# Decoder megakernel on one core: clearing the semaphores of a stage late and together instead of after every stage

## The reference

```
x = x + L0_attn(layernorm(x))    # linear attention and a lookup MLP
x = x + L0_xattn(layernorm(x), ctx, mask)
x = x + L0_ffn(layernorm(x))     # 8 experts, top 2
x = x + L1_attn(layernorm(x))    # gated scan
x = x + L1_xattn(layernorm(x), ctx)
x = x + L1_ffn(layernorm(x))     # quantised weights and activations
x = x + L2_attn(layernorm(x))    # gated delta rule
x = x + L2_xattn(layernorm(x), ctx, ctx, mask)
x = x + L2_ffn(layernorm(x))     # 64 experts, top 8
x = x + L3_attn(layernorm(x))    # causal softmax attention, 16 heads
x = x + L3_xattn(layernorm(x), ctx, ctx)
x = x + L3_ffn(layernorm(x))     # up to 3 steps with a top-k mask
```

## Time and profile before

| | |
|---|---|
| median of three runs | 2252.6 us (2238.38 to 2256.27) |
| profiled execution | 2238.47 us, of which the span of the program's instructions is 2236.3 us |
| TensorE matmul (PE) busy | 1937.9 us, 87% |
| VectorE (DVE) busy | 1415.2 us, 63% |
| ScalarE (ACT) busy | 1161.3 us, 52% |
| GpSimd (POOL) busy | 825.1 us, 37% |
| mean granted TensorE clock | 0.914 of full speed |
| DMA | 107.45 MB, mean 48 GB/s |

### The profile page before, as it was taken

The page is one execution under the profiler, slowest core; times in us unless marked ns, Lnnn a source line. Parts: engine busy times, 40 slices in busy tenths (PEclk is TensorE's granted clock), DMA queues, the critical chain, the costliest instruction groups (busy, mean ns, idle before and its releaser), DMA issues. The chain is left out here.

```text
span 2236.3 us, 51051 instructions
## 1 busy us (share of the span) xinstructions
PE 1937.9 (87%) x20208; PEld 1377.7 (62%) x20208; DVE 1415.2 (63%) x2462; ACT 1161.3 (52%) x2407; POOL 825.1 (37%) x1071
## 2 busy tenths in 40 slices
PE   4888999967435899999999978799999989999786
PEld 2335787843123588888888863688778856633332
DVE  3645887864463567777777433688777766944434
ACT  3445555553454766666666435455555552056452
POOL 0002454510000566665666410476666640034200
PEclk8998999987555999999999989899999988989998
DMA  6000100100000310000000012344434420000100
GB/s 272 1 1 1 58 29 29 38 1 0 1 0 1 125 48 13 22 22 13 22 13 22 22 74 108 100 131 129 131 113 123 132 57 1 1 1 1 43 1 20
DMA packets 31952, 107.45 MB, mean 48 GB/s; under 512 B 9440, under 2 KB 9568, under 8 KB 30816
## 3 DMA queue, kind: packets, MB, share of 16 engines
q1 hardware_dynamic: 30624, 104.01, 14.0%
q10 hardware_dynamic: 1088, 0.13, 0.0%
HBM read 94.10 MB, written 10.03 MB: 47 GB/s over the span
## 5 line engine op out<-in xcount | busy, mean ns | idle before, releaser
L599 PE MATMUL bank<-yh,wl 128*128 128x512 f32 x640 | 253.9, 397 | 16.5 <-DVE yl L1214 6.8
L600 PE MATMUL bank<-yl,wh 128*128 128x512 f32 x640 | 252.3, 394 | 0.0
L601 PE MATMUL bank<-yh,wh 128*128 128x512 f32 x640 | 252.2, 394 | 0.0
L1781 DVE SCALAR_TENSOR_TENSOR big<-bank,pack,big 128x256 f32<-128x256 f32 (+2 forms) x384 | 182.2, 477 | 34.1 <-ACT mask L1703 17.0
L1267 DVE TENSOR_TENSOR hl<-bank,hh 128x512 fp32r<-128x512 f32 x192 | 132.8, 692 | 69.1 <-ACT hh L1204 59.6
L1702 ACT ACTIVATE big<-bank,pack 128x256 f32<-128x256 f32 x192 | 91.0, 474 | 133.9 <-PE bank L1537 133.1
L1204 ACT ACTIVATE hh<-bank 128x512 fp32r<-128x512 f32 x192 | 115.1, 599 | 76.0 <-DVE bank L1262 75.8
L599 PEld LDWEIGHTS bank<-yh,wl 128*128 128x128 f32 x640 | 122.1, 191 | 51.7 <-issue 16.2
L687 ACT ACTIVATE a<-bank,pack 128x512 f32<-128x512 f32 x128 | 88.4, 691 | 105.4 <-PE bank L601 105.4
L1262 DVE TENSOR_TENSOR bank<-bank,a 128x512 f32<-128x512 f32 x192 | 133.3, 694 | 8.2 <-POOL a L1143 1.4
L601 PEld LDWEIGHTS bank<-yh,wh 128*128 128x128 f32 x640 | 121.9, 190 | 26.2
(11 more groups left out here) (469 smaller groups left out, 4608.1 us busy)
## 6 DMA issues: line engine op xcount, KB each, us to landing
rep<-routing SPq DMA_DIRECT2D x64, 384.0 KB, 3.4
rep<-routing SPq DMA_DIRECT2D x64, 256.0 KB, 4.0
big<-in_big SPq DMA_DIRECT2D x1, 9216.0 KB, 25.7
rep<-routing SPq DMA_DIRECT2D x16, 512.0 KB, 3.5
gate<-big SPq DMA_DIRECT2D x32, 256.0 KB, 2.0
z<-gate SPq DMA_DIRECT2D x16, 512.0 KB, 3.4
rep<-routing SPq DMA_DIRECT2D x64, 128.0 KB, 3.4
big<-in_big SPq DMA_DIRECT2D x1, 6144.0 KB, 34.3
```

Source lines behind the costliest of these rows:

```text
L599: nc.tensor.matmul(out, pl, dh[:, cur], start=start, stop=False)
L600: nc.tensor.matmul(out, ph, dl[:, cur], start=False, stop=False)
L601: return nc.tensor.matmul(out, ph, dh[:, cur], start=False, stop=stop)
L1781: ins = nc.vector.scalar_tensor_tensor(out=d, in0=conv_in(i, back), scalar=weight(i, 3 - back), in1=d, op0=ALU.mult, op1=ALU.add)
```

## The change

Stages no longer clear. Their semaphores are collected in a list. When the list holds more than 80, all of them are cleared and freed and one barrier follows, and the list is emptied. `program` calls the same function once more at its very end.

```diff
+counted = []
+
+
 class Kit:
     pass
 
 
+def zero(nc):
+
+    nc.clear_and_free_semaphores(counted)
+    nc.all_engine_barrier()
+    counted.clear()
...
     with nc.Block() as block:
         yield block, sems
-    nc.clear_and_free_semaphores(list(sems.values()))
-    nc.all_engine_barrier()
+    counted.extend(sems.values())
+    if len(counted) > 80:
+        zero(nc)
...
 def program(nc, ap, out, cols, first, last):
+    counted.clear()
     with ExitStack() as mem:
...
             @block.sync
             def _(sp):
                 sp.wait_ge(k.big_loaded, 48)
+        zero(nc)
```

## The result

Six executions of the changed kernel took 2207.45 to 2239.51 us, median 2211.44 us; the kernel before took 2223.98 to 2256.27 us beside it, median 2241.89 us. The ratio is 0.9889, with a 95% interval from 0.9842 to 0.9937. The kernel is faster by 1.1%, where 0.37% was forecast, and the median lies outside the range of 2229 to 2256 us.

What follows compares the result with a forecast made beforehand. PE, busy 87% of the span, bounds the stages, but everything between a stage end's two releases is on the path. Removing 23 barriers (8.7 us) and adding one (0.4 us) takes 8.3 us off 2252.6: 2244 us, range 2229 to 2256.

Steps and rivals of the forecast that it cites:

- The price of a barrier: At each stage end, release to release: a clear of n names with its barrier costs 0.38 + 0.007 n us.
- the sum: Over all stage ends: 23 barriers removed, 8.7 us, one added at the program's end, 0.4 us; net gain 8.3 us.
- clears at double price: At the five remaining clears: if larger clears cost double, 2.4 us more in all, leaving a gain of 5.9 us.
- the base: Starting time of the whole kernel: the median of three runs, 2252.6 us, from which the 8.3 us were taken.
- So I cost the move itself at nothing: Behind each stage end: the next stage's work moves forward with the release, no transfer was hidden, so the shift costs 0.
- The rival of the clock: At stage boundaries: less idle time keeps TensorE's clock up, ten norms win 15 us more, 2229 us; chance 0.06.
- The rival on the other side: In long stages' openings: low-clock stretches move into dense matmuls, some 4 us each, three give 2256 us; chance 0.10.
- The rival without effect: At each stage's start: instruction fetch makes first instructions late by what was saved, 2253 us; chance 0.06.

Runs made afterwards that it cites:

- barrier_kept: The changed kernel with one barrier of all engines put back at each stage's end, clears still together: ratio to the kernel before 1.0023, mean 2247.9 us.
- kept_22_23: The changed kernel with the barrier kept only before and behind the norm in front of the causal attention: ratio to the kernel before 0.9944, mean 2228.5 us.
- kept_late: The changed kernel with the barrier gone at the first 18 stage ends and kept at the last 10: ratio to the kernel before 0.9883, mean 2226.6 us.
- fill_after: The changed kernel with matmuls that nothing reads added in the ten norm stages: ratio to the kernel before 0.9931, mean 2227.2 us.
- kept_early: The changed kernel with the barrier kept at the first 18 stage ends and gone at the last 10: ratio to the kernel before 0.9926, mean 2228.6 us.
- before_again: The kernel before with no edit, run against itself and profiled a second time: ratio 1.0002.

## Why the prediction was wrong

**The price of a barrier was right.** 0.38 + 0.007 n us for a pair held beyond the names that had been read (1.0 us with 98). Five clears, one barrier at the end, gaps of 0.5 us: all as forecast. At an equal clock the sum nearly stands too: 5.9 us, give or take 2, where 8.3 us was forecast, and 10.4 us for the 28 barriers of barrier_kept, where 10.6 us was read. One small slip: clears at double price would add 2.6 us for 474 names at 5.5 ns, not 2.4; nothing hangs on it.

**Some 10 us of the miss are the base.** The forecast started from the median of three runs, 2252.6 us. The mean of 75 executions of the kernel before is 2242.5 us, so the three were a high draw. With the base at 2242.5 the forecast would have been 2234 us, and the changed kernel's mean of 2216.3 us would still be 18 us below it. That part is not luck.

**The step that failed is "So I cost the move itself at nothing".** It looked for transfers that the barrier might have covered, and found none; nor did any show in the runs. But to take 0.4 us out of the stage ends changed at which level TensorE ran the stages, and this term, put at nothing, measured some 20 us. The mean clock rose from 0.913 to 0.923, worth 20 us at the slope found above; with 6 us at equal clock that is the 26 us between the means (2242.5 us over 75 executions of before that ran beside these kernels, 2216.3 over twelve).

**The rival of the clock had the right sign and the wrong chance and price.** I gave it 0.06, with 15 us. Its argument against, that 0.38 us is small beside tails of up to 12.9 us, compared lengths, where the level of a whole short stage can change with the shift: the second norm of layer0 went from a mean clock of 0.87 to 1.00, the projections from 0.62 to 0.75, for 0.4 us. In another profile without these barriers (kept_22_23) the same norm took 12.2 us at 0.88, so even there it is no certain gain. The norms, from which I took its price, are not where most of it was: all ten took 163.4 us before and 158.1 us in the changed kernel, their barriers included. I had the causal attention in hand, as a price for a loss of some 4 us in an opening; in fact the clock falls again and again in its first 95 us, which ran at a mean of 0.98 in the changed kernel and of 0.68 in kept_late, and this costs 10 to 25 us, since VectorE is the bound at the one level and PE at the other.

**The rival on the other side** claimed that shifts win as often as they lose. For one kernel against another no run here refutes that; but in the first 18 stages the effect goes with the code (five profiles against five, 10.6 us or more apart) and is not drawn anew in each execution, as the length of the causal attention of the kernel before is. Here it fell on the good side in both places: 9.6 to 12.3 us for the first 18 stage ends, of which 6.8 us are barriers, and 12.2 us for two more, of which 0.8 us are. That both were good is luck, as far as is known.

**The rival without effect** is gone: the next work came 0.1 us after the release as before. PE's branch took 3516 ns in place of the 3859 ns of the earlier trace rows, ScalarE's again 50 ns, so the code's new place changed little:

```profile
L2435 PEldq COMPARE_BRANCH  x1: 3516/3516/3516, 2209.5 to 2209.5; - x1
...
L2447 ACTq COMPARE_BRANCH  x1: 50/50/50, 2209.6 to 2209.6; - x1
```

**What stays open:** why the causal attention falls into its short form after the shorter boundary; what makes the clock fall after a stretch in which PE was 98% busy; the second heap of fill_after; and whether it is the barrier's time or its instructions that count, for no run delayed the stages by other means.

## What to carry to other kernels

Read the price of a barrier from release to release; it adds up as read. But where TensorE alternates between its two levels, take a shift of some tenths of a microsecond at a stage's start as a change of its own, with a range as wide as the kernel's own scatter on both sides of the structural sum, and look for the stage whose bound changes with the level. To judge such a change, compare executions at the same granted clock as well as medians: the one difference is the structure's, the other the clock's. And take several profiles of each kernel and of its neighbours: two that agree to 0.2 us can do so by luck, as they did here, while five against five told a gain of 12 us from a scatter of 1.5 us.

## What the runs showed of the hardware

A range clear of semaphores took 45 ns for 2 names, 347 ns for 57 and 565 ns for 98, 5.3 to 5.5 ns for each name more, with a DRAIN of 192 ns in front of the last, where it was 62 to 144 ns with up to 57. One program on one core ran between 2223.94 and 2261.22 us with mean clocks of 0.921 and 0.905. The same 2208 weight loads and matmuls of the causal attention kept PE busy for 237 us at a clock of 0.95 (kept_early) and for 263 us at 0.85 (kept_late), and the stage grew by 0.45 us for each us at the low level. The clock fell after 16.8 us at the full level in which PE was busy for 16.43 us (before_again), and stayed up through the same stretch with 16.56 us (kept_early). Matmuls added to keep PE active in the norms raised the mean clock to 0.932 and made the kernel slower by 8 to 11 us.
